# A two-layer sparse graph network: a shallower pipeline, early products and an earlier flag

## The reference, cut to what matters

```python
h = relu(layernorm(x))
node_att = softmax(h @ node_w, axis=0)          # over all nodes
e = (h @ edge_w) @ (h @ edge_w).T
edge_att = softmax(where(adj > 0, e, NEG_BIG), axis=1)
x = x + (adj * node_att * edge_att) @ (h @ weight) + bias
h = relu(layernorm(x))
A_ = adj + eye;  d = rsqrt(A_.sum(axis=1))
x = x + relu((A_ * d[:, None] * d[None, :]) @ h @ W)
```

## Time and profile before

| | us |
|---|---|
| median of 3 runs (lowest to highest) | 745.87 (741.02 to 753.41) |
| the profiled execution, its own time | 738.04 |
| its span, first to last instruction | 736.3 |
| mean granted TensorE clock, share of full speed | 0.814 |

### The profile page before, as it was taken

One profiled execution on the slowest core, in us unless ns is written; L12 is line 12 of the kernel. 1 busy time (PEld: TensorE's weight loads), 2 busy tenths in 40 slices (PEclk: granted clock), 3 DMA queues, 4 the chain that ended last, 5 costly groups with the idle time before them and its releaser, 6 DMA issues.

```text
span 736.3 us, 9790 instructions
## 1 busy us (share of the span) xinstructions
PE 509.3 (69%) x2630; PEld 424.7 (58%) x2630; DVE 414.5 (56%) x2162; ACT 299.1 (41%) x566; POOL 345.2 (47%) x347
## 2 busy tenths in 40 slices
PE   2467777777778787777776589356676565776783
PEld 1256555765767675666675479344555454665662
DVE  4845466675765785667675577443333453454542
ACT  5784347455457464585563335301111111111111
POOL 0015323564556464564554630275455557456650
PEclk9979877897888797989797878657777898688887
DMA  9997435674775675687631311232222234233331
GB/s 279 409 385 284 146 141 170 248 281 160 270 246 206 234 273 186 242 276 258 200 134 45 114 30 58 78 103 85 78 87 84 83 92 115 71 93 97 104 101 45
DMA packets 39085, 121.26 MB, mean 165 GB/s; under 512 B 7700, under 2 KB 25566, under 8 KB 34932
## 3 DMA queue, kind: packets, MB, share of 16 engines
q1 hardware_dynamic: 18772, 80.62, 29.9%
q0 software_dynamic: 16080, 35.80, 16.8%
q10 hardware_dynamic: 4176, 4.19, 1.6%
HBM read 116.13 MB, written 12.58 MB: 175 GB/s over the span
## 4 chain that ended last, share of the span: by engine, by line
PE 42%; DVE 21%; another core or an unknown queue 15%; issue 12%; ACT 7%; DMA 1%; POOL 0%; DVEq 0%; ACTq 0%; POOLq 0%
PE z L1046 9%; PE lists L1115 4%; PE code L989 4%; PE code L1007 4%; PE g_rows L1115 3%; PE o L979 2%; DVE prod L480 2%; PE by_row L979 2%; PE o L1056 2%; PE g_rows L1022 2%; PE lists L1016 2%; DVE C L393 2%; ACT A L838 2%; PE lists L1110 2%
## 5 line engine op out<-in xcount | busy, mean ns | idle before, releaser
L330 POOL DMA_INDIRECT HJ<-h_rows,NBR x192 | 200.3, 1043 | 225.6 <-DVE NBR L467 133.4
L339 POOL DMA_INDIRECT HJ<-h_rows,NBR x96 | 93.8, 977 | 66.2 <-DMA h_rows<-G 37.3
L819 ACT ACTIVATE junk<-A 128x2048 bf16<-128x2048 f32 x64 | 122.0, 1906 | 1.0
L1046 PEld LDWEIGHTS z<-DG,HJ 128*128 128x128 f32 x768 | 119.6, 242 | 3.8
L1046 PE MATMUL z<-DG,HJ 128*128 128x128 f32 x768 | 117.6, 324 | 0.0
L1007 PE MATMUL code<-LST,A 128*128 128x42 f32 x216 | 40.0, 344 | 81.2 <-DVE A L656 64.9
L1007 PEld LDWEIGHTS code<-LST,A 128*128 128x128 f32 x216 | 36.1, 249 | 92.8 <-DVE A L656 74.8
L989 PE MATMUL code<-A,POW 128*128 128x256 bf16 x512 | 74.0, 293 | 16.4 <-issue 16.3
L345 POOL DMA_INDIRECT HJ<-h_rows,A x47 | 49.1, 1044 | 72.0 <-DVE A L671 61.4
L989 PEld LDWEIGHTS code<-A,POW 128*128 128x128 bf16 x512 | 48.8, 101 | 35.1 <-issue 22.0
L480 DVE CUSTOM_DVE_ANT_0 prod<-G,HJ 128x256 f32<-128x256 f32 x160 | 66.2, 418 | 0.0
(11 more groups left out here) (189 smaller groups left out, 1043.6 us busy)
## 6 DMA issues: line engine op xcount, KB each, us to landing
A<-in_adj_dram SPq DMA_DIRECT2D x32, 2048.0 KB
HJ<-h_rows,NBR POOLq DMA_INDIRECT x288
X<-in_x_dram SPq DMA_DIRECT2D x4, 1024.0 KB, 11.0
h_rows<-G SPq DMA_DIRECT2D x4, 1024.0 KB, 7.6
out_dram<-junk SPq DMA_DIRECT2D x32, 128.0 KB
h_rows<-G ACTq DMA_DIRECT2D x3, 1024.0 KB
h_rows<-G ACTq DMA_DIRECT2D x1, 768.0 KB
HJ<-h_rows,A POOLq DMA_INDIRECT x47, 3.1
```

The source lines that it names most:

```text
L330: g.indirect_dma_start(out=HJ[:, t % SLOTS, c, :], out_offset=None, in_=table0, in_offset=bass.IndirectOffsetOnAxis(ap=NBR[:, t, c:c + 1], ...
L339: g.indirect_dma_start(out=HJF[:, t % DRING * K2 + k, :], out_offset=None, in_=table1, in_offset=bass.IndirectOffsetOnAxis(ap=NBR[:, t, k: ...
L819: checked.by(S_.activation(junk[:], A[:, t % ABUF, j * (N // 2):(j + 1) * (N // 2)], ACT.Square, accum_out=SQ[:, t, j:j + 1]))
L1046: mm = MM(bZ[:, d * P:(d + 1) * P], HJ[:, t % SLOTS, c, d * P:(d + 1) * P], DG[:, t % 2, c, :], start=c == 0, stop=c == CH - 1)
```

## The change

The loop of stage one is one turn shorter (T + 6), and almost every step runs one turn earlier relative to its tile: scores of i-2 for i-3, masks and weights of i-3 for i-4, `weighted` and `keep_z` of i-4 for i-5, but `attended` on PE stays at i-5 and thus lies a turn behind `weighted`. On PE `codes(i+3)` moves from behind `weighted` to a place right after `to_edges(i)`; on DVE `top` and `clear` move into the scores, `rest` ahead of the statistics. Twelve tiles of early products are made before turn 0, then seven in each of turns 0 and 1 and six in turn 2; the node softmax is in turns 3 and 4. The bias is added in turns 4 to 7 instead of 0 to 3. The copies of the edge products and the powers of two move from DVE to ACT, the zeroing of the ring `HJ` from ACT to POOL.

In stage two distances are made two turns ahead, rows one; the identity product is replaced by an addition on DVE (`own2`); `gathered_sum` comes last in PE's turn. The flag is computed during the last turns of stage one without POOL, and the two parts share one block, so that the barrier between them and POOL's drain go away. Several semaphores are merged.

```diff
-EARLY = 2
-PER_I = 8
-ZTURN = 4
+EARLY = 12
+PER_I = 7
+ZTURN = 3
...
 POOL
+            g.memset(HJ[:].rearrange("p s c d -> p (s c d)"), 0.0).then_inc(c_hj, 1)
...
-            g.wait_ge(end_d, 7)
-            g.partition_all_reduce(zs[:, 7:8], zs[:, 6:7], P, RMAX).then_inc(end_p, 1)
...
 DVE, before the turns
-                    for k in range(NBLK):
-                        ins = V.tensor_scalar(POW[:, k, :], ident[:], float(BLK << k), None, ALU.mult)
...
+                if n < BATCH:
+                    for t in range(4 * n, 4 * n + 4):
+                        keep_ht(t)
...
 DVE, a turn
+                if f:
+                    top(i + LEAD)
                 if w:
+                    direct_score(i - 2, 4)
+                if f:
+                    clear(i + LEAD)
+                if w:
+                    edge_score(i - 2)
...
+                if f:
+                    rest(i + LEAD)
+                if z:
+                    attended(i - 5)
...
                 if i + 1 < T:
                     rows_matrix(i + 1)
...
+                if 0 <= i - 4 < NGRP:
+                    add_bias(i - 4)
+                if 0 <= i - T - 1 < AHEAD:
+                    rows2(i - T - 1)
...
+                if i == T + 2:
+                    flag_rows()
+                if i == T + 4:
+                    flag_all()
...
 DVE, stage two
             for t in range(T + 3):
-                if t + AHEAD < T:
-                    rows2(t + AHEAD)
                 if t < T:
                     v.wait_ge(gd[t % DRING], 16 * K2 * (t // DRING + 1))
-                    sum2a.by(V.tensor_tensor(YA[:, t % 2, :], HJF[:, t % DRING * K2, :], HJF[:, t % DRING * K2 + 1, :], ALU.add))
+                    own2.by(V.tensor_tensor(YD[:, t % 2, :], G[:, t, 0:D], HJF[:, t % DRING * K2, :], ALU.add))
+                    sum2a.by(V.tensor_tensor(YA[:, t % 2, :], HJF[:, t % DRING * K2 + 1, :], HJF[:, t % DRING * K2 + 2, :], ALU.add))
...
                 if t + 1 < T:
                     edges2(t + 1)
+                if t + AHEAD + 1 < T:
+                    rows2(t + AHEAD + 1)
...
 ACT, before the turns
+            for k in range(NBLK):
+                ins = S_.activation(POW[:, k, :], ident[:], ACT.Relu, scale=float(BLK << k))
...
+                for j in range(2):
+                    if n == 0:
+                        for t in range(4 * j, 4 * j + 4):
+                            g_keep(t)
+                    if n == 1 and j == 0:
+                        distance(0)
+                        for t in range(8, EARLY):
+                            g_keep(t)
+                    squares(n, j)
...
 ACT, stage two
-                if t + AHEAD + 1 < T:
-                    distance2(t + AHEAD + 1)
+                if t + AHEAD + 2 < T:
+                    distance2(t + AHEAD + 2)
...
 PE, a turn
                 if i < T:
                     to_edges(i)
...
+                for t in late(i)[0:2]:
                     turn0(t)
                 if i + LEAD < T:
                     codes(i + LEAD)
+                if 0 <= i - 2 < T:
+                    g_edges(i - 2)
+                if 0 <= i - 3 < T and i < T:
+                    to_weights(i - 3)
                 if i % BATCH == BATCH - 1 and i + 1 < T:
                     prefixes((i + 1) // BATCH)
...
+                if 0 <= i - 5 < T:
+                    attended(i - 5)
+                for t in late(i):
+                    product0(t)
+                    if t + 2 in late(i):
+                        turn0(t + 2)
+                if 0 <= i - 4 < T:
+                    weighted(i - 4)
...
+                if 0 <= i - 2 < T:
+                    by_row(i - 2)
...
 PE, stage two
-                MM(bY[t % 2][:, 0:D], ident[:], G[:, t, 0:D], start=True, stop=False)
...
                 if t + AHEAD < T:
                     to_edges2(t + AHEAD)
-                if t < T:
-                    gathered_sum(t)
                 if 0 <= t - 1 < T:
                     turn1(t - 1)
                 if 0 <= t - 2 < T:
                     convolved(t - 2)
+                if t < T:
+                    gathered_sum(t)
...
 the end
+        block = ctx.enter_context(nc.Block(no_gpsimd_drain=True))
```

More of the change, by code:

```diff
@@ L84, in wait, with edge_path @@
         eng.wait_ge(self.sem, t * self.per + (self.per if k is None else k))
-def edge_path(nc, flag, x, adj, w0, bias, node_w, edge_w, w1, out, table0, table1):
+def edge_path(nc, block, signals, flagged, flag, x, adj, w0, bias, node_w, edge_w, w1, out, table0, table1):
     adj_t = adj.rearrange("(t p) n -> t p n", p=P)
@@ L731, in _ @@
[L731 to L747 removed]
+                        diagonal(i - 3, k)
@@ L751, in _ @@
                     rows_matrix(i + 1)
+                if z:
+                    means1(i - 5)
+                for t in late(i)[4:]:
+                    keep_ht(t)
+                for n, (_, b) in enumerate(GROUPS):
+                    if b == i - 4:
+                        norm_a(n)
+                if 0 <= i - 4 < NGRP:
+                    add_bias(i - 4)
+                if 0 <= i - T - 1 < AHEAD:
+                    rows2(i - T - 1)
+                for n, (_, b) in enumerate(GROUPS):
+                    if b == i - (5 if b < T else 4):
+                        norm_b(n)
@@ L878, in _ @@
             for n in range(LEAD):
[L879 to L884 removed]
+                for j in range(2):
[7 more added lines that the diff above has]
+                    squares(n, j)
             def node_exp(i):
                 if i == ZTURN:
[L888 to L889 removed]
+                    a.wait_ge(node, 5)
+                    S_.activation(NATT[:], G[:, :, D], ACT.Exp, bias=zs[:, 2:3], accum_out=zs[:, 3:4]).then_inc(node, 1)
             made = 0
             ready = 0
[L893 removed]
+            for i in range(T + 6):
                 f = i + LEAD < T
@@ L896, in _ @@
                     squares(i + LEAD, 0)
-                if 0 <= i - 4 < T:
-                    exponent(i - 4)
-                    for k in range(ADIAG):
-                        diagonal(i - 4, k)
-                if 0 <= i - 5 < T:
-                    keep_z(i - 5)
-                for t in late(i):
-                    g_keep(t)
-                node_exp(i)
-                if i + 1 < T and (i + 1) % BATCH > 0:
-                    distance(i + 1)
-                if f and i < 3:
-                    squares(i + LEAD, 0)
-                if f:
-                    squares(i + LEAD, 1)
+                if 0 <= i - 3 < T:
+                    exponent(i - 3)
+                    for k in range(ADIAG):
+                        diagonal(i - 3, k)
+                if late(i):
+                    distance(i + 1)
+                    for t in late(i)[0:2]:
+                        g_keep(t)
+                    if i < 3:
+                        squares(i + LEAD, 0)
+                    for t in late(i)[2:3]:
+                        g_keep(t)
+                    squares(i + LEAD, 1)
+                    for t in late(i)[3:]:
+                        g_keep(t)
+                node_exp(i)
+                if not late(i) and f:
+                    squares(i + LEAD, 1)
+                if not late(i) and i + 1 < T:
+                    distance(i + 1)
+                if 0 <= i - 4 < T:
+                    keep_z(i - 4)
                 for _ in range(3 if i + LEAD >= T else 1):
@@ L1132, in convolved @@
                 o1_ps.by(mm)
-            h1.wait(pe, T - 1)
             for t in range(T + 2):
@@ L1161, in link, with general_path @@
         eng.wait_ge(self.sem, self.at(turn, self.n))
-def general_path(nc, flag, x, adj, w0, bias, node_w, edge_w, w1, out, table):
+def general_path(nc, block, flagged, flag, x, adj, w0, bias, node_w, edge_w, w1, out, table):
     adj_t = adj.rearrange("(t p) n -> t p n", p=P)
```

309 lines of the change are left out of this document (150 added, 159 removed).

## The result

The changed kernel takes 690.52 us, median of 4 runs (681.94 to 699.23), beside 743.44 (737.81 to 753.41) before: a ratio of 0.927, 95% interval 0.914 to 0.941. The forecast was 671 with 638 to 715. The profiled execution took 681.94 us with a span of 680.2, 56.1 less than the one before.

A forecast was written before the change was run, and what follows sets the result against it. No engine was busy over 69%, so chains between engines were taken to bound the kernel. Savings of 10 + 19 + 7 + 32 + 6 = 74 us from 738.04 gave 664, times 1.011 is 671, range 638 to 715.

The forecast's parts named there:

- Turns 4 to 30: Stage one's later turns: early codes shorten a turn from 11.4 to 10.7 us, set by gathers; 19 us saved, bounds 0 to 51.
- The signs: Expected trace marks: 10.7 us turns, no DVE wait for codes, PE's rows-matrix wait well below 59.6, stage two some 36 us earlier.
- my bound of 9.5: Shortest stage-one turn allowed from turn 4 on: DVE's 7.5 us with 2 of waits, that is 51 us saved.
- Stage two: Its 32 turns: distance two ahead and rows one ahead shorten each from 7.9 to 6.9 us; 32 saved, bounds 5 to 55.
- Hence not 47 but 1.0 a turn, 32: Stage two: lookahead removes 1.48 us between relu and lists, 47 in all, cut to 32 because POOL is late next.
- Gathers hold PE in both stages: Rival, chance 0.20: PE can't end a turn before the sixth gather; stage one stays 11.4, stage two saves 16; 707 us.
- Turns 0 to 3: Start of stage one: twelve tiles of products leave these turns at 0.8 us each; 10 saved, bounds 3 to 16.
- the 12.5 of my upper bound: Length in us assumed for each of turns 1 to 3 in the best case, giving the upper bound of 16 saved.
- the wait for the load that I had named: Turn 0: codes 3 wait for load 3, which early products push back by 3 to 6 us.
- Before turn 0: The 48.4 us ahead of stage one's turns: powers move to ACT, zeroing to POOL; nothing saved, bounds -3 to +3.
- Drain and end: Drain: one turn less, 7 us saved (0 to 12); end: one barrier and POOL's drain go, 6 saved (3 to 8).
- The Trainium skill's rule on shared ports: Two-input VectorE and SBUF-reading GpSimd instructions block each other: bias costs 2 us in four turns, new additions 13 in stage two.

The follow-up runs named there:

- e1: Changed kernel with ACT's exponent and its diagonals ahead of the first half of the squares in stage one; 683.2 us, 0.952 of before.
- e2: Changed kernel with two of the six gathers of each stage-one turn left out, so part of the result is missing; 633.7 us, one run.
- d2: Changed kernel with the codes back behind the weighted product in PE's turn from turn 3 on, DVE and ACT keeping their new order; 835.2 us, 1.139 of before.
- c1: The changed kernel run again without an edit, in a set where the kernel before took 613.0 us; 572.9 us, 0.933 of before.
- the second set: Four profiled runs with their own kernel before (613.0 us): changed kernel again, stop for the product, fill between gathers, half rows; 572.6 to 583.5 us.
- d1: Changed kernel with stage two's lookahead undone: distance one turn ahead, rows matrix in the turn that needs it; 689.7 us, 0.934 of before.
- e3: Changed kernel with both stage-one edits: exponent ahead of the squares and four gathers a turn instead of six; 626.9 us, one run.
- e4: Changed kernel with one wait added: in stage two GpSimd starts turn t's direct gathers only after PE's sum of turn t-2; 666.3 us, 0.934 of before.
- d3: Changed kernel with exponent first, GpSimd's stage-two wait for the sum two turns back, and its stage-one stop for the product after three gathers; 646.5 us, 0.878.
- the half rows: Changed kernel with all gathers of both stages fetching 128 elements instead of 256, the same number of gathers and descriptors; 572.6 us, one run.
- The kernel with the stop: Changed kernel with exponent first, paced stage two, and GpSimd waiting behind its third stage-one gather for the product; run twice: 583.5 us (0.953), 646.5 us (0.878).

## Why the prediction was right, and where it was not

**Turns 4 to 30: right, for the reason given.** I took the turn for the gathers with what leads to them and what follows (10.7; measured 10.63 in turn 15, 10.78 in the mean with its few longer turns). e1 (PE's product earlier, nothing gained in plain turns) and e2 (two gathers less, 1.8 us gained) show it. The signs came: turns 14 to 20 take 10.61 to 10.75 us each, with a decode or without; DVE's wait for the codes, 3.79 us in the earlier trace rows, is gone from the turn; PE's wait for the rows matrix is 0.9; the first gather of stage two came 33.9 us earlier (439.53) where I said 36. That the measured 0.6 a turn is due to the codes alone was not shown: d2 says that without them early the new order is 5 us a turn worse.

The reason holds only where PE is held behind the gathers. In c1 they are as long and the turn is 8.4, below my bound of 9.5; there both kernels are 118 to 130 us faster than in the result, and 671 would have been far off. That the profile of before and the result were both taken with the hold is luck, and so is the nearly equal ratio of the second set (0.933): the time saved there is 40 us, and no profile of the kernel before shows where.

**Stage two: within the bounds, but not by the mechanism.** The step that failed is "Hence not 47 but 1.0 a turn, 32". The stretch gave 17.4, and the lookahead for which the 1.0 stood gave nothing that can be told from the spread: without it (d1) stage two is 241.4 us long, with it (changed kernel, e1, e2, e3, d2) 236.1 to 245.9. POOL's wait for lists fell from 61.4 to 36.1, not to half, and a turn is 7.4, not 6.9. That the sum lay within 5 to 55 is luck. So is that it lies near the 16 of the rival "Gathers hold PE in both stages", which halved the same term. That rival has the mechanism, PE held while POOL runs, and e4 shows it; its other half, no gain in stage one, did not come about, since the turn had 0.6 us of other things to lose. What made the 17.4 is not separated: PE's work in stage two fell from 172.0 to 140.8 us with the identity product gone, and the sum comes last in its turn; neither was tried alone.

**Turns 0 to 3: 16.7 instead of 10.** The term was worked out with a wrong count: ten tiles left the turns (30 late ones before, 20 now), not twelve, so by its own price of 0.8 a tile it should have been 8. Most of the surplus lies in turns 1 to 3, which took 11.9 each, under the 12.5 of my upper bound. Turn 0 with 17.0 was long, with the wait for the load that I had named. The changed kernel there:

```profile
49.43 0.28 PE L1028 MATMUL lists<-CUM,below 128*128 128x2 f32 x2
...
50.48 0.29 DVE L451 TENSOR_SCALAR R<-DIST,HALF 128x128 f32<-128x128 f32 x1 [0.31 <-ACT DIST L844]
...
52.99 0.31 PE L1047 MATMUL lists<-LST,R 128*128 128x40 f32 x2
...
57.50 0.28 PE L1018 MATMUL code<-iota_row,ones_row 1*128 1x256 bf16 x1 [3.74 <-DMA A<-in_adj_dram]
```

**Before turn 0: -3.8, outside my bounds.** The first three rows are the step that I missed. PE's prefixes, which distance 0 waits for, start at 49.43, behind early products (44.62 before), and the rows matrix starts 2.45 us later than before (50.48, 48.03). DVE has it at 50.77, but PE's lists come 2.2 us later, behind the last of the twelve early products; before, they followed at once. Work put into an engine's idle time was put ahead of the first thing that the others wait for.

**Drain and end** came to 9.3 of 13. The end is 4.54 us where I had said under 4; in the other profiles of changed kernels it is 2.9 to 5.1.

**The Trainium skill's rule on shared ports (SBUF — State Buffer, Who interferes with whom)** showed in single gathers and not in the sum. The fifth gather of turn 4 lay beside the bias:

```profile
113.52 3.02 POOL L332 DMA_INDIRECT HJ<-h_rows,NBR  x1 [0.30 <-issue]
```

Yet turns 4 to 7 took 9.9 us in the mean, less than the 10.6 behind them, and the 143 gathers of stage two took 142.6 us beside 142.9 before, in spite of 32 new additions.

## What to carry to other kernels

Find out which engine's results come late although its rows have ended, and what the last thing to run before them was; an edit that moves work on the held engine may then gain nothing, and one on the engine that holds it may gain. A wait can make a pipeline faster: where the hold was, GpSimd running some 20 us ahead of PE cost more than stopping it. Test an order edit together with the order of the engine that it feeds. Take the control from the same set, and look at single turns beside the mean: in e1 two effects of opposite sign made a zero. Repeat a set before trusting a chain that may not be there the next time.

## What the hardware showed that I had not expected

In two of the three sets, and in the profile of the changed kernel, PE's weighted product came 1.0 to 1.2 us after the end of an unbroken run of GpSimd's indirect gathers (0.97, 1.04, 1.15 us in e1, d3 and the changed kernel), 3.95 us after PE's rows ended in d3. That is the rule and not three chosen turns: in turns 8 to 30 of the changed kernel ACT took the product 1.1 to 1.3 us after the sixth gather in 19 of 23, in c1 while a gather was running in 20 of 23. But not all of PE's results are held. In turn 15 of the changed kernel DVE had PE's prefixes at 227.57, 0.04 us after their rows ended and in the middle of the gathers; and in the kernel before, where the product lies earlier in PE's turn, it came while a gather was running in 17 of 23 turns. In stage two the lateness grew along a run to 12.6 us, and DVE waited 10.38 us for one sum, with the granted clock at 0.50 (1.2 GHz) for the last five of them, in which PE's rows show no work:

```profile
513.00:518.00 5.00, 0.00 (x0) 0.00 (x0) 0.00 (x0) 0.95 (x2) 2.63 (x3) 0.50 0.37 105
```

In the other set there was none of it, and the kernel before took 613 us instead of 720 to 743, the changed one 573 instead of 690. The gathers' own lengths were the same in both (median 1.00 us), and the chip was the same in the second set and the third. Why the hold is there at one time and not at another, which of PE's work it touches, and whether descriptors or bytes make it, stays open: the half rows ran where there was no hold. The kernel with the stop is 5% faster than the changed one with the hold and 2% slower without it; pacing stage two costs nothing without it (190.4 beside 191.5), and helps with it.
